# Rotary embedding with the sine ahead of the swap, and fixed PSUM bank pairs for even and odd score tiles and for the row maxima, in the order maximum, scores, scores, maximum

## The chip, the cores and the metric

The program runs on one core of one Trainium2 chip. The metric is the device time of one launch in microseconds (us). TensorE (PE) multiplies and writes to PSUM; VectorE (DVE), ScalarE (ACT) and GpSimd (POOL) do the elementwise work; SyncE (SP) issues the DMAs. Each engine works through its own instructions in order and waits on semaphores that the others count up.

## The reference

A block of two expert layers with attention between them, on x of 8 x 1024 tokens x 256 in float32:

```python
x = x + 0.5 * ffn(layernorm(x))          # 8 experts, top 2, and a shared one
x = x + attention(layernorm(x))
x = x + 0.5 * ffn(layernorm(x))
```

The change touches the attention alone:

```python
c_q, c_kv = h @ w_down_q.T, h @ w_down_kv.T               # 256 -> 128
q, k, v = (c @ w_up.T for each)                            # 16 heads of 64
e, o = xr[..., 0::2], xr[..., 1::2]                        # q and k, all 64 dimensions
rot = stack([e * cos - o * sin, e * sin + o * cos], -1)
attn = softmax(einsum('bhqd,bhkd->bhqk', q, k) / 8)
out = einsum('bhqk,bhkd->bhqd', attn, v) @ w_out.T + residual
```

## The kernel before, in words

Three blocks follow each other: `ffn`, `attention`, `ffn`. In the attention the work goes by pairs of heads, n = 0 to 63 (8 batches x 8 pairs). The rows of a pair's two heads lie on partitions 0 to 63 and 64 to 127, so a product over the 64 dimensions of a head uses half of the array and both heads run beside each other. "Even" and "odd" below are even and odd n.

A pair takes 8 periods, r = 0 to 7. `order` (L701 to L713) writes all steps of all engines in one list, and each engine takes from it those that concern it. Steps that belong to the beginning, the early part, the late part or the end of a period are put there by `at` (L661 to L699). A period holds:

- two score tiles (L894), here s0 and s1, each 128 keys x 512 queries x 2 heads, six row pairs of matmuls in all: the float32 product is made of three products of high and low parts;
- two maxima tiles (L873), here m0 and m1, of the pair that comes next: 128 queries x 512 keys x 2 heads from the high parts alone. DVE takes the row maximum (L1072). The maxima of 512 queries become a row, go to DRAM and back broadcast (`SH`), and are filled into a PSUM bank pair (L1001 on ACT, L1078 on DVE for every fourth tile) ahead of the scores, which add onto them;
- ACT's exponential of each score tile (L1010, `grown`), then two products with V (L905, attends, of the period before), and POOL's sums of exponentials (L1170);
- one or two other steps that share the single bank `OT`: raise (L852, the up projection of q or k, four per pair, in periods 2 to 5, for the pair two ahead or so), value (L864, periods 1 and 6), row (L880, periods 1 and 5), sum (L927, periods 2 and 6), and outward (L945, the output projection). Outward steps stand in odd pairs only: two in period 0, early and late, and one late in periods 3 and 4. Turn and latent (L834, L842) prepare the next batch; the last latent stands late in period 0 of one even pair per batch.

The rotation, one half of q or k at a time: PE raises into `OT`; ACT copies `OT` to `R` (L984); DVE multiplies `OT` by the cosine into `U` (L1049), and waits for ACT's copy first; two DMAs write `R` to `VT` with even and odd rows exchanged; POOL multiplies `VT` by the signed sine (L1149, "sine", end of the next period); DVE adds it to `U` (L1062, "rotate", late in the period after that). When all four are in, ACT makes the high parts `KH` (early in period 0) and `QH` (end of period 0) (L990), POOL the low part of k (L1160), DVE the low part of q, `QL` (L1067, end of period 1).

Score and maxima tiles share three bank pairs `PS0` to `PS2` in turn, in the order in which they stand: `ring = Banks(3, ...)` (L805). Each use takes the pair that the use three before it had, and waits until that one was read: a score tile by its exponential, a maxima tile by its row maximum. PE's wait is in `take`:

```python
before = ring.before[use]
if before:
    pe.wait_ge(*(grown if before[0] == "score" else most_out)(*before[1:]))
```

In the order s0, s1, m0, m1 the use three before m1 is s0 of the same period.

Of the kernel before, what the change touches and what calls it, by code (L numbers as in the profile page):

```python
# [5 lines left out]
class Once:  # L6


    def __init__(self, eng):
        self.eng, self.seen = eng, {}  # L10
# [7 lines left out]
class Signal:  # L18
# [14 lines left out]
    def past(self, *key):  # L33

        return self.sem, self.at.get(key, 0)

# [9 lines left out]
def macaron_kernel(nc, a, out):  # L46
# [557 lines left out]
    def attention(src, dst, held):  # L604
        with ExitStack() as local:
# [3 lines left out]
            def sig(name, by=1):  # L609
                return Signal(ctx.enter_context(nc.semaphore("at" + name)), by)  # L610
# [10 lines left out]
            U = sb("U", [128, 2, S], fp32)  # L621
# [92 lines left out]

            def events(*names):
                return [step[1:] for step in order if step[0] in names]
# [30 lines left out]
            sined, rotated = (sig(x).expect(events("rotate")) for x in ("sined", "rotated"))  # L747
# [47 lines left out]
            def place(use):  # L795
                return room.get(use, OT[:, :])
# [8 lines left out]
            ring = Banks(3, [s for s in order if s[0] in ("score", "most")])  # L805

            def tensor(pe):
# [6 lines left out]
                def take(use):  # L814

                    before = ring.before[use]
                    if before:
                        pe.wait_ge(*(grown if before[0] == "score" else most_out)(*before[1:]))
                    else:
                        for i in (2 * ring.of[use] + 6, 2 * ring.of[use] + 7):  # L820
                            pe.wait_ge(*FREED[first[i][0]](*first[i][1:]))
                    return PS[ring.of[use]]
# [127 lines left out]
            def scalar(act):  # L950
                for step in order:
# [26 lines left out]
                    elif name == "raise":  # L978
                        _, n, i, t = step
                        k, before = swap_of(n, i, t)  # L980
                        act.wait_ge(*raised(n, i, t))
                        if before:
                            act.wait_ge(*swapped[k](*before))
                        act.eng.activation(R[k][:, :], place(step), ACT.Copy).then_inc(raw.sem)  # L984
# [11 lines left out]
                    elif name == "fill" and filler(step[3]) < 2:  # L996
                        _, n, t, j = step
                        before = ring.before[("score", n, t, j)]
                        act.wait_ge(*shift[t](n))
                        act.wait_ge(*(grown if before[0] == "score" else most_out)(*before[1:]))  # L1000
# [23 lines left out]
            def vector(dve):  # L1024
                for step in order:
# [16 lines left out]
                    elif name == "raise":  # L1042
                        _, n, i, t = step
                        sl = slice(t * 512, (t + 1) * 512)
                        dve.wait_ge(*raw(n, i, t))
                        dve.wait_ge(*ups(1))
                        dve.wait_ge(*high.past(n - 1, i))
# [8 lines left out]
                    elif name == "rotate":  # L1056
                        _, n, i, t = step
                        sl = slice(t * 512, (t + 1) * 512)
                        k, before = swap_of(n, i, t)
# [13 lines left out]
                    elif name == "fill" and filler(step[3]) == 2:  # L1073
                        _, n, t, j = step
                        before = ring.before[("score", n, t, j)]
                        dve.wait_ge(*shift[t](n))
                        dve.wait_ge(*(grown if before[0] == "score" else most_out)(*before[1:]))
# [34 lines left out]
            def gpsimd(pool):  # L1112
# [3 lines left out]
                for step in order:  # L1116
# [27 lines left out]
                    elif name == "sine":  # L1144
                        _, n, i, t = step
                        k, before = swap_of(n, i, t)
                        pool.wait_ge(*ups(1))
                        pool.wait_ge(*swapped[k](n, i, t))
                        pool.eng.tensor_tensor(VT[k][:, :], VT[k][:, :], SIN[:, t * 512:(t + 1) * 512], ALU.mult).then_inc(sined.sem)  # L1149
# [160 lines left out]
```

## Time and profile before

| | |
|---|---|
| median of 3 runs | 4203.93 us (4203.29 to 4210.23) |
| profiled execution | 4204.82 us, span 4202.9 us |
| TensorE clock, mean granted | 0.986 |
| busy: PE, DVE, ACT, POOL | 94%, 71%, 66%, 72% of the span |
| attention stage, 1200 to 2200 us | PE 949, DVE 757, ACT 726, POOL 824 us busy |
| DVE row maxima L1072 | x1024, 1220 ns each |
| DVE rotate L1062 | x256, 1385 ns each in the larger group |
| POOL sine L1149 | x254 in the larger group, 1303 ns each |
| ACT copy to R L984 | x252, 597 ns each |

The busy share of PE is modelled at its ends; in the timeline the start of one matmul and the start of the next tell more than the durations. A row of the timeline holds several instructions of one kind when they follow each other.

### The profile page before, as it was taken

The page shows a single profiled execution, that of the slowest core. Times are in us where ns is not written, and L with a number is a line of the kernel's source. Part 1 is how long each engine was busy: PE and PEld are TensorE (multiplying, and loading weights), DVE is VectorE, ACT ScalarE, POOL GpSimd, SP SyncE. Part 2 cuts the span into 40 slices and gives each one's busy share as a digit, 9 for nine tenths or more (in the row PEclk, how much of TensorE's full clock was granted, in tenths as well). Part 3 has the DMA queues.
Part 4 walks back from the last instruction along what each step waited for, and adds up shares of the span by engine and source line. Part 5 has one row for each costly group of instructions (what it writes and reads, how often), then busy time and mean ns, then how long its engine had stood idle before and what let it go on. Part 6 is the DMA issues. An engine that isn't in the chain of part 4 may idle for free. (4 is left out here: it accounts for less than half of the span.)

```text
span 4202.9 us, 66226 instructions
## 1 busy us (share of the span) xinstructions
PE 3943.4 (94%) x24908; PEld 2235.9 (53%) x24908; DVE 2964.9 (71%) x3709; ACT 2769.4 (66%) x3532; POOL 3018.6 (72%) x1634
## 2 busy tenths in 40 slices
PE   7999979999999999999999999999999999989999
PEld 6888834444444444444444444444444444468888
DVE  5656568777777776877777777777777877555563
ACT  4444457777777777777777777777776777744544
POOL 3444458888888887888788788888887888734443
PEclk9999989999999999999999999999999999999999
DMA  3333221112211211121122112111211121133331
GB/s 110 106 121 112 73 91 54 57 54 67 71 52 52 79 54 52 60 78 51 52 65 69 53 56 81 52 51 59 74 55 57 58 72 62 42 110 105 121 111 61
DMA packets 192775, 300.39 MB, mean 71 GB/s; under 512 B 50327, under 2 KB 100936, under 8 KB 191816
## 3 DMA queue, kind: packets, MB, share of 16 engines
q1 hardware_dynamic: 192456, 296.17, 21.9%
q8 instruction: 196, 3.21, 0.3%
q14 instruction: 123, 1.01, 0.1%
HBM read 201.20 MB, written 26.73 MB: 54 GB/s over the span
## 5 line engine op out<-in xcount | busy, mean ns | idle before, releaser
L1072 DVE TENSOR_REDUCE atNM<-atPS 128x2 f32<-128x1024 f32 x1024 | 1208.0, 1220 | 568.5 <-PE atPS L873 563.0
L1170 POOL TENSOR_TENSOR atACC<-atACC,atPT 128x1024 f32<-128x1024 f32 x510 | 1277.2, 2504 | 69.0 <-ACT atPT L1010 15.0
L1010 ACT ACTIVATE atPT<-atPS 128x1024 f32<-128x1024 f32 x1024 | 995.3, 1022 | 197.3 <-PE atPS L894 187.3
L905 PE MATMUL atPO<-atPT,atV 128*64 128x512 f32 x4096 | 972.5, 595 | 0.0
L1001 ACT ACTIVATE atPS<-atSH 128x1024 f32<-128x1024 f32 x768 | 767.5, 1023 | 39.7 <-DMA atSH<-atMD 24.9
L1170 POOL TENSOR_TENSOR atACC<-atPT 128x1024 f32<-128x1024 f32 x255 | 624.7, 2450 | 105.7 <-PE atOT L927 102.8
L873 PE MATMUL atPS<-atKH,atQH 64*128 64x512 f32 x2048 | 456.5, 448 | 124.0 <-ACT atPT L1010 112.3
L1149 POOL TENSOR_TENSOR atVT<-atVT,atSIN 128x512 f32<-128x512 f32 x254 | 331.0, 1303 | 295.9 <-DMA atVT<-atR 295.9
L905 PEld LDWEIGHTS atPO<-atPT,atV 128*64 128x64 f32 x4096 | 281.6, 137 | 472.9 <-issue 466.6
L894 PE MATMUL atPS<-atQH,atKL 64*128 64x512 f32 x2048 | 469.0, 454 | 38.0 <-ACT atPS L1001 35.2
L894 PE MATMUL atPS<-atQH,atKH 64*128 64x512 f32 x2048 | 405.3, 391 | 0.0
L894 PE MATMUL atPS<-atQL,atKH 64*128 64x512 f32 x2048 | 404.7, 391 | 0.0
L894 PEld LDWEIGHTS atPS<-atQH,atKL 64*128 64x128 f32 x2048 | 191.8, 184 | 381.9 <-ACT atPS L1001 174.1
L873 PEld LDWEIGHTS atPS<-atKH,atQH 64*128 64x128 f32 x2048 | 193.7, 185 | 364.9 <-ACT atPT L1010 321.0
L523 POOL TENSOR_TENSOR f2GL<-f2GF,f2GH 128x512 fp32r<-128x512 f32 x144 | 200.6, 1395 | 254.2 <-ACT f2GH L368 254.2
L523 POOL TENSOR_TENSOR f1GL<-f1GF,f1GH 128x512 fp32r<-128x512 f32 x144 | 198.4, 1381 | 251.0 <-ACT f1GH L368 249.4
L1062 DVE TENSOR_TENSOR atU<-atU,atVT 128x512 f32<-128x512 f32 x254 | 351.7, 1385 | 20.6 <-POOL atVT L1149 20.6
L1078 DVE COPY atPS<-atSH 128x1024 f32<-128x1024 f32 x256 | 311.4, 1217 | 11.2 <-ACT atPT L1010 11.2
L984 ACT ACTIVATE atR<-atOT 128x512 f32<-128x512 f32 x252 | 150.5, 597 | 182.5 <-PE atOT L852 182.5
L945 PE MATMUL atOT<-atWO,atAT 128*64 128x256 f32 x1984 | 239.8, 384 | 1.1 <-POOL atAT L1155 1.1
L476 DVE TENSOR_TENSOR f2GF<-f2HB,f2GB 128x512 f32<-128x512 f32 x128 | 101.6, 794 | 182.0 <-ACT f2HB L362 131.7
L1022 ACT ACTIVATE atRSUM<-atOT 128x512 f32<-128x512 f32 x126 | 75.4, 598 | 234.0 <-PE atOT L927 234.0
(280 smaller groups left out, 6835.9 us busy)
## 6 DMA issues: line engine op xcount, KB each, us to landing
atSH<-atMD SPq DMA_DIRECT2D x128, 512.0 KB, 4.5
atVT<-atR SPq DMA_DIRECT2D x508, 128.0 KB, 2.1
f1GB<-f1GD SPq DMA_DIRECT2D x128, 256.0 KB, 7.2
f2GB<-f2GD SPq DMA_DIRECT2D x128, 256.0 KB, 6.9
atRSUM<-atRD SPq DMA_DIRECT2D x126, 256.0 KB, 4.0
X<-x SPq DMA_DIRECT2D x4, 1024.0 KB, 6.0
XS<-x SPq DMA_DIRECT2D x16, 256.0 KB, 3.9
x<-X SPq DMA_DIRECT2D x16, 256.0 KB, 2.7
```

Of the source, the lines that this page charges most:

```text
L523: pool.eng.tensor_tensor(GL[n % NH][:, :], GF32[n % NH][:, :], GH[n % NH][:, :], ALU.subtract).then_inc(low_h.sem)
L873: ins = pe.eng.matmul(bank[:, h, :], QH[n % 2][HI[h], q * 128:(q + 1) * 128], KH[n % 2][HI[h], t * 512:(t + 1) * 512], start=True, stop=True)
L894: ins = pe.eng.matmul(bank[:, h, :], kk[HI[h], keys], q[HI[h], sl], start=False, stop=k == 2, skip_group_check=True)
L905: ins = pe.eng.matmul(PO[HI[h], :], V[n % 2][:, j, HI[h]], PT[k % NPT][:, h, :], start=j == 0, stop=j == T - 1)
L945: ins = pe.eng.matmul(place(step)[HI[c], i * D:(i + 1) * D], AT[:, (n - GP + 1 + q) % NAT, tok:tok + 64], WO[:, (p - GP + 1 + q) * D:(p - ...
L1001: act.eng.activation(PS[ring.of[("score", n, t, j)]][:, :, :], SH[t][:, :, :], ACT.Copy).then_inc(filled[filler(j)].sem)
L1010: act.eng.activation(PT[k % NPT][:, :, :], PS[ring.of[step]][:, :, :], ACT.Exp, scale=SCALE).then_inc(grown.sem)
L1062: dve.eng.tensor_tensor(U[:, i, sl], U[:, i, sl], VT[k][:, :], ALU.add).then_inc(rotated.sem)
L1072: dve.eng.tensor_reduce(NM[:, q // 4, :, q % 4, t], PS[ring.of[step]][:, :, :], AX.X, ALU.max, negate=True).then_inc(most_out.sem)
L1078: dve.eng.tensor_copy(PS[ring.of[("score", n, t, j)]][:, :, :], SH[t][:, :, :]).then_inc(filled[2].sem)
L1149: pool.eng.tensor_tensor(VT[k][:, :], VT[k][:, :], SIN[:, t * 512:(t + 1) * 512], ALU.mult).then_inc(sined.sem)
L1170: pool.eng.tensor_tensor(total[:, :, :], begun[:, :, :], PT[k % NPT][:, :, :], ALU.add).then_inc(gathered.sem)
```

## The change

Two edits, independent of each other.

The rotation: DVE multiplies `OT` by the sine straight into `R` (in ACT's place), then `OT` by the cosine into `U`; the swap follows; POOL subtracts `VT` from `U` ("rotate", at the end of the period after the raise, where "sine" stood). The sign of the table goes with the row it is multiplied in, hence the subtraction. ACT's copy, the step "sine" and DVE's addition are gone.

The banks: even score tiles always use `PS0`, odd ones `PS1`, maxima `PS2`. Each use waits for the last reader of its own pair. The order in a period becomes m0, s0, s1, m1.

```diff
+class Kept:
+    def __init__(self, of):
+        self.of, self.before, last = of, {}, {}
+        for use, bank in of.items():
+            self.before[use] = last.get(bank)
+            last[bank] = use
...
-                    at(end, m, k - 5, ("sine", m, i, t))
-                    at(late, m, k - 4, ("rotate", m, i, t))
+                    at(end, m, k - 5, ("rotate", m, i, t))
...
-                order += begin.get(g, []) + scores + mosts + early.get(g, []) + fills + attends
+                order += begin.get(g, []) + mosts[:1] + scores + mosts[1:] + early.get(g, []) + fills + attends
...
-            ring = Banks(3, [s for s in order if s[0] in ("score", "most")])
+            ring = Kept({s: s[3] % 2 if s[0] == "score" else 2 for s in order if s[0] in ("score", "most")})
+            def cleared(use):
+                before = ring.before[use]
+                if before:
+                    return [(grown if before[0] == "score" else most_out)(*before[1:])]
+                return [FREED[x[0]](*x[1:]) for x in first[6:] if first.index(x) // 2 - 3 == ring.of[use]]
...
-                    elif name == "raise":            # scalar
-                        _, n, i, t = step
-                        k, before = swap_of(n, i, t)
-                        act.wait_ge(*raised(n, i, t))
-                        if before:
-                            act.wait_ge(*swapped[k](*before))
-                        act.eng.activation(R[k][:, :], place(step), ACT.Copy).then_inc(raw.sem)
...
                     elif name == "raise":            # vector
-                        dve.wait_ge(*raw(n, i, t))
+                        k, before = swap_of(n, i, t)
+                        dve.wait_ge(*raised(n, i, t))
                         dve.wait_ge(*ups(1))
+                        if before:
+                            dve.wait_ge(*swapped[k](*before))
+                        dve.eng.tensor_tensor(R[k][:, :], place(step), SIN[:, sl], ALU.mult).then_inc(raw.sem)
                         dve.wait_ge(*high.past(n - 1, i))
                         dve.wait_ge(*(klow if i else qlow).past(n - 1))
                         dve.eng.tensor_tensor(U[:, i, sl], place(step), COS[:, sl], ALU.mult).then_inc(cosine.sem)
...
-                    elif name == "rotate":           # vector
-                        dve.wait_ge(*sined(n, i, t))
-                        dve.wait_ge(*cosine(n, i, t))
-                        dve.eng.tensor_tensor(U[:, i, sl], U[:, i, sl], VT[k][:, :], ALU.add).then_inc(rotated.sem)
...
-                    elif name == "sine":             # gpsimd
-                        pool.wait_ge(*swapped[k](n, i, t))
-                        pool.eng.tensor_tensor(VT[k][:, :], VT[k][:, :], SIN[:, t * 512:(t + 1) * 512], ALU.mult).then_inc(sined.sem)
+                    elif name == "rotate":           # gpsimd
+                        pool.wait_ge(*swapped[k](n, i, t))
+                        pool.wait_ge(*cosine(n, i, t))
+                        pool.eng.tensor_tensor(U[:, i, sl], U[:, i, sl], VT[k][:, :], ALU.subtract).then_inc(rotated.sem)
```

TensorE around the border of periods 0 and 1 of an even pair. `KH0,atQH0` is the pair whose maxima end, `KH1,atQH1` the next one, whose high parts are made in period 0. Before:

```order
L873 MATMUL atPS1<-atKH0,atQH0 128x512 x2
L873 MATMUL atPS2<-atKH0,atQH0 128x512 x2
L905 MATMUL atPO<-atPT4,atV1 64x512 x2
L905 MATMUL atPO<-atPT5,atV1 64x512 x2
L894 MATMUL atPS0<-atQH0,atKL0 128x512 x2
L894 MATMUL atPS0<-atQL0,atKH0 128x512 x2
L894 MATMUL atPS0<-atQH0,atKH0 128x512 x2
L894 MATMUL atPS1<-atQH0,atKL0 128x512 x2
L894 MATMUL atPS1<-atQL0,atKH0 128x512 x2
L894 MATMUL atPS1<-atQH0,atKH0 128x512 x2
L873 MATMUL atPS2<-atKH1,atQH1 128x512 x2
L873 MATMUL atPS0<-atKH1,atQH1 128x512 x2
```

The same place after the change (the maxima are L885 there, the attends L917, the scores L906, the value step L876):

```order
L885 MATMUL atPS2<-atKH0,atQH0 128x512 x2
L917 MATMUL atPO<-atPT0,atV1 64x512 x2
L917 MATMUL atPO<-atPT1,atV1 64x512 x2
L885 MATMUL atPS2<-atKH1,atQH1 128x512 x2
L906 MATMUL atPS0<-atQH0,atKL0 128x512 x2
L906 MATMUL atPS0<-atQL0,atKH0 128x512 x2
L906 MATMUL atPS0<-atQH0,atKH0 128x512 x2
L906 MATMUL atPS1<-atQH0,atKL0 128x512 x2
L906 MATMUL atPS1<-atQL0,atKH0 128x512 x2
L906 MATMUL atPS1<-atQH0,atKH0 128x512 x2
L885 MATMUL atPS2<-atKH1,atQH1 128x512 x2
L876 MATMUL atOT<-atWV,atCKV1 64x128 x8
```

The first maxima tile of the next pair moved from behind the six score products of period 1 to in front of them, and both maxima tiles of a period lie in `PS2`.

VectorE from period 0 to period 2 of an even pair, before (L1078 is a fill, L1083 the step "minus", L1054 the copy of V):

```order
L1078 COPY atPS2<-atSH0 128x1024
L1083 TENSOR_REDUCE atMC<-atNM 128x8
L1072 TENSOR_REDUCE atNM<-atPS0 128x2
L1072 TENSOR_REDUCE atNM<-atPS1 128x2
L1054 COPY atV1<-atOT 128x512
L1067 TENSOR_TENSOR atQL1<-atU,atQH1 128x1024
L1072 TENSOR_REDUCE atNM<-atPS1 128x2
L1072 TENSOR_REDUCE atNM<-atPS2 128x2
L1049 TENSOR_TENSOR atU<-atOT,atCOS 128x512
L1078 COPY atPS1<-atSH0 128x1024
```

And after the change:

```order
L1080 COPY atPS1<-atSH0 128x1024
L1085 TENSOR_REDUCE atMC<-atNM 128x8
L1074 TENSOR_REDUCE atNM<-atPS2 128x2 x2
L1063 COPY atV1<-atOT 128x512
L1069 TENSOR_TENSOR atQL1<-atU,atQH1 128x1024
L1074 TENSOR_REDUCE atNM<-atPS2 128x2 x2
L1055 TENSOR_TENSOR atR0<-atOT,atSIN 128x512
L1058 TENSOR_TENSOR atU<-atOT,atCOS 128x512
L1080 COPY atPS1<-atSH0 128x1024
```

The order is the same but for the sine product in front of the cosine product; `QL` still stands right ahead of period 2's two row maxima.

## Rows read from the trace of the kernel before

**Rows 1.** The page: busy time, share and instructions of each engine.

```profile
PE 3943.4 (94%) x24908; PEld 2235.9 (53%) x24908; DVE 2964.9 (71%) x3709; ACT 2769.4 (66%) x3532; POOL 3018.6 (72%) x1634
```

**Rows 2.** Waits of the whole span: waiter, releaser, us in total, times, longest.

```profile
PEld atPS L873 <- ACT atPT L1010: 321.0, 504, 1.3
```

**Rows 3.** Timeline, period 3 of an odd pair: start, duration, engine, line, idle before.

```profile
2107.05 0.50 PE L894 MATMUL atPS<-atQH,atKL 64*128 64x512 f32 x2
...
2108.54 0.40 PE L873 MATMUL atPS<-atKH,atQH 64*128 64x512 f32 x2
...
2108.98 2.36 DVE L1072 TENSOR_REDUCE atNM<-atPS 128x2 f32<-128x1024 f32 x2 [2.08 <-PE atPS L873]
2109.12 0.51 PE L873 MATMUL atPS<-atKH,atQH 64*128 64x512 f32 x2 [0.19 <-ACT atPT L1010]
2109.56 1.08 PE L852 MATMUL atOT<-atCKV,WK 128*64 128x512 f32 x4
...
2110.47 1.89 PE L905 MATMUL atPO<-atPT,atV 128*64 128x512 f32 x8
...
2111.32 0.69 DVE L1049 TENSOR_TENSOR atU<-atOT,atCOS 128x512 f32<-128x512 f32 x1
2112.19 1.90 PE L945 MATMUL atOT<-atWO,atAT 128*64 128x256 f32 x16
...
2114.01 0.50 PE L894 MATMUL atPS<-atQH,atKL 64*128 64x512 f32 x2
2114.13 0.69 DVE L1110 TENSOR_TENSOR XS<-XS,atOT 128x512 f32<-128x512 f32 x1 [2.12 <-PE atOT L945]
```

**Rows 4.** Timeline, a maxima tile that is first in its run, and its reader.

```profile
2049.99 0.51 PE L873 MATMUL atPS<-atKH,atQH 64*128 64x512 f32 x2
```

```profile
2050.53 2.36 DVE L1072 TENSOR_REDUCE atNM<-atPS 128x2 f32<-128x1024 f32 x2 [5.05 <-PE atPS L873]
```

**Rows 5.** Timeline of DVE, then of PE: periods 4 and 5, even pair.

```profile
2070.70 1.22 DVE L1078 COPY atPS<-atSH 128x1024 f32<-128x1024 f32 x1
...
2073.24 0.18 DVE L1097 TENSOR_REDUCE atRI<-atRQ 128x16 f32<-128x32 f32 x1
...
2073.64 2.35 DVE L1072 TENSOR_REDUCE atNM<-atPS 128x2 f32<-128x1024 f32 x2
```

```profile
2072.77 0.74 PE L873 MATMUL atPS<-atKH,atQH 64*128 64x512 f32 x4
2073.44 1.08 PE L852 MATMUL atOT<-atCQ,WQ 128*64 128x512 f32 x4
...
2076.65 0.27 PE L880 MATMUL atOT<-ident,atMC 128*8 128x128 f32 x1 [0.41 <-DVE atU L1049]
```

**Rows 6.** The line of QL: ns min/median/max, first and last start; then timeline rows.

```profile
L1067 DVE TENSOR_TENSOR atQL<-atU,atQH x64: 1215/2824/3435, 558.7 to 3605.3; 128x1024 fp32r<-128x1024 f32 x64
```

```profile
2146.90 2.96 DVE L1067 TENSOR_TENSOR atQL<-atU,atQH 128x1024 fp32r<-128x1024 f32 x1
```

```profile
2146.40 2.37 POOL L1170 TENSOR_TENSOR atACC<-atPT 128x1024 f32<-128x1024 f32 x1
```

**Rows 7.** The group of QL over the span: count, busy us, mean ns.

```profile
L1067 DVE TENSOR_TENSOR atQL<-atU,atQH 128x1024 fp32r<-128x1024 f32 x64 | 166.5, 2602 | 0.0
```

**Rows 8.** Timeline of ACT, then of PE: periods 7, 0 and 1.

```profile
2135.69 1.98 ACT L1001 ACTIVATE atPS<-atSH 128x1024 f32<-128x1024 f32 x2
2138.04 1.94 ACT L1010 ACTIVATE atPT<-atPS 128x1024 f32<-128x1024 f32 x2 [0.38 <-PE atPS L894]
...
2142.23 1.07 ACT L990 ACTIVATE atQH<-atU 128x1024 fp32r<-128x1024 f32 x1
```

```profile
2132.65 0.50 PE L894 MATMUL atPS<-atQH,atKL 64*128 64x512 f32 x2
...
2144.69 1.09 PE L864 MATMUL atOT<-atWV,atCKV 128*64 128x128 f32 x16
```

**Rows 9.** The page's costliest groups: DVE's addition of the rotation, mean ns.

```profile
L1062 DVE TENSOR_TENSOR atU<-atU,atVT 128x512 f32<-128x512 f32 x254 | 351.7, 1385 | 20.6 <-POOL atVT L1149 20.6
```

More of the change, by code:

```diff
@@ L746, in attention @@
             swapped = [sig(f"swap{k}", 32).expect([s for s in events("raise") if swap_of(*s)[0] == k]) for k in range(4)]
-            sined, rotated = (sig(x).expect(events("rotate")) for x in ("sined", "rotated"))
+            rotated = sig("rotated").expect(events("rotate"))
             high = sig("high").expect(events("high"))
@@ L814, in take @@
                 def take(use):
-                    before = ring.before[use]
-                    if before:
[L818 to L821, printed above, removed]
+                    for event in cleared(use):
+                        pe.wait_ge(*event)
                     return PS[ring.of[use]]
@@ L977, in scalar @@
                         act.eng.activation(C[b % 2][i][:, t * 512:(t + 1) * 512], place(step), ACT.Copy).then_inc(latent_out.sem)
-                    elif name == "raise":
-                        _, n, i, t = step
-                        k, before = swap_of(n, i, t)
-                        act.wait_ge(*raised(n, i, t))
-                        if before:
-                            act.wait_ge(*swapped[k](*before))
-                        act.eng.activation(R[k][:, :], place(step), ACT.Copy).then_inc(raw.sem)
                     elif name == "high":
@@ L997, in scalar @@
                         _, n, t, j = step
-                        before = ring.before[("score", n, t, j)]
                         act.wait_ge(*shift[t](n))
-                        act.wait_ge(*(grown if before[0] == "score" else most_out)(*before[1:]))
+                        for event in cleared(("score", n, t, j)):
+                            act.wait_ge(*event)
                         act.eng.activation(PS[ring.of[("score", n, t, j)]][:, :, :], SH[t][:, :, :], ACT.Copy).then_inc(filled[filler(j)].sem)
@@ L1055, in vector @@
                                             OT[:, :].rearrange("p (i d) -> p i d", d=128)).then_inc(value_out.sem)
-                    elif name == "rotate":
-                        _, n, i, t = step
-                        sl = slice(t * 512, (t + 1) * 512)
-                        k, before = swap_of(n, i, t)
-                        dve.wait_ge(*sined(n, i, t))
-                        dve.wait_ge(*cosine(n, i, t))
-                        dve.eng.tensor_tensor(U[:, i, sl], U[:, i, sl], VT[k][:, :], ALU.add).then_inc(rotated.sem)
                     elif name == "qlow":
@@ L1074, in vector @@
                         _, n, t, j = step
-                        before = ring.before[("score", n, t, j)]
                         dve.wait_ge(*shift[t](n))
-                        dve.wait_ge(*(grown if before[0] == "score" else most_out)(*before[1:]))
+                        for event in cleared(("score", n, t, j)):
+                            dve.wait_ge(*event)
                         dve.eng.tensor_copy(PS[ring.of[("score", n, t, j)]][:, :, :], SH[t][:, :, :]).then_inc(filled[2].sem)
@@ L1143, in gpsimd @@
                             then(10, pool.eng.tensor_tensor(B[:, two], A[:, two], NG[:, :], ALU.mult))
-                    elif name == "sine":
+                    elif name == "rotate":
                         _, n, i, t = step
+                        sl = slice(t * 512, (t + 1) * 512)
                         k, before = swap_of(n, i, t)
-                        pool.wait_ge(*ups(1))
                         pool.wait_ge(*swapped[k](n, i, t))
-                        pool.eng.tensor_tensor(VT[k][:, :], VT[k][:, :], SIN[:, t * 512:(t + 1) * 512], ALU.mult).then_inc(sined.sem)
+                        pool.wait_ge(*cosine(n, i, t))
+                        pool.eng.tensor_tensor(U[:, i, sl], U[:, i, sl], VT[k][:, :], ALU.subtract).then_inc(rotated.sem)
                     elif name == "divide":
```

## The prediction, made before the changed kernel ran

> **What bounds the kernel now.** I read the busy line first: PE is busy for 94% of the span, the other engines for at most 72% [rows 1]. Then the waits, for what PE waits for inside the attention: the line that stands out is the second maxima tile, held by ACT's exponential before 504 of its weight loads [rows 2]. Then the timeline of single periods. There PE is a chain without holes but for this one. Period 3 of an odd pair [rows 3] runs: s0 at 0 (2107.05), m0 at 1.49, m1 at 2.07, raise at 2.51, attends at 3.42, outward at 5.14, the next s0 at 6.96. m0 follows the score product before it at the usual 0.23 (six products and the entry of 0.1 make 1.49), but m1 follows m0 by 0.58. Two dense maxima are 0.23 apart: in period 5 of an even pair m0 and m1 together take 2073.44 - 2072.77 = 0.67 until the raise [rows 5], and the raise comes 0.44 after m1 in either case [rows 3]. So each of the 512 periods can lose 0.35 on the shared bank pair, 180 us in all. DVE, ACT and POOL have slack; what matters is whether each is on time for PE in the new order.
>
> **The wait that goes, and the one that comes.** After the change m1 waits for DVE's row maximum of m0, since both lie in PS2. From m0 = 0: m0 is now first in its run behind another kind of matmul; such a tile reaches DVE 0.54 after its start (2049.99 to 2050.53) [rows 4], against 0.44 when it is not first [rows 3]. A row maximum takes 1.22 (two in 2.36, the second starts after 1.18). A release reaches PE after 0.06. m1 can start at 0.54 + 1.22 + 0.06 = 1.82; its place by the order alone is 0.33 + 6 x 0.23 = 1.71. The step behind it then starts at 2.25 or 2.26, not 2.51. So an undisturbed period gains 0.26, not 0.35. For every 0.1 that DVE comes later than 0.54 to m0, PE loses 0.1; from 0.8 on the period is longer than before. Before, DVE could come late by a whole tile without PE noticing, since both maxima came last and their pairs were wanted again only a period later.
>
> So the question is what DVE does at the start of a period. Its list per raise period is: maximum, maximum (next step 1.17 after the second's start), sine product, cosine product (0.60 each to the next step, as the one with the cosine now, 0.69 in itself), fill (1.13) in every second period. The sine product reads OT in PSUM as the cosine product does, so I price it at the same row. The second maximum starts at 1.82 + 0.54 = 2.36, the sine at 3.53, the cosine at 4.13, OT is free at 4.82, a fill ends DVE's list at 5.86. PE: raise 2.25, attends 3.16 (0.91 on), next s0 or m0 at 4.98 without a late step; with outward, which wants OT, 4.88 by the order and 5.00 by OT (0.18 from the cosine's end, as 2111.32 + 0.69 to 2112.19), so there 0.12 of the gain is gone.
>
> **Period by period** (plus is slower; per pair of heads).
> - Periods 3 and 4 of even pairs and period 6 of all: DVE on time. -0.26 each, 128 periods: -33 us.
> - Period 7, for 39 of 64 pairs (the others below): -10 us.
> - Periods 3 and 4 of odd pairs: period 3 -0.26 + 0.12. In period 4 the addition of the outward step before comes first, 0.12 after the period's border for 0.60 (2114.01 to 2114.13) [rows 3]: maximum at 0.72, m1 at 2.00, +0.18, with the 0.12 of OT that is +0.05. Together -0.09 x 32: -3 us.
> - Period 5, odd: addition until 0.72, then the sums' inverse and "minus", 0.40 from 2073.24 to 2073.64 [rows 5] and some 0.6 where a release is late, say 0.45: maximum at 1.17, m1 at 2.45, next step 2.88 against 2.51: +0.37 x 32 = 12 us.
> - Period 5, even: the fill ends at 5.86, 0.88 into the period, inverse and minus to 1.33, m1 at 2.61, next step 3.04: +0.53. But before, PE already lost 0.4 to 0.5 in many of these, as the row waited for OT (2076.65) [rows 5]; there DVE still had its addition L1062 ahead of the maxima. I put that old loss at 0.35 on the mean of the 32, which leaves +0.18, 6 us.
> - Period 2, all pairs: QL stands ahead of m0's maximum. It starts 1.06 ahead of the border (m1 of period 1 at 1.82, V copied by 4.1, the border at 5.2). It takes 1.2 to 3.4, mean 2.60 [rows 6, 7]. The row of 2146.90 shows why: POOL's sum runs until 2148.77 and QL ends at 2149.86, 1.09 after it [rows 6]; QL does its 1.2 us of work when POOL's instruction is through. At the mean it ends at 1.47, m1 starts at 2.75, the next step at 3.18, against 2.51 and some 0.09 that a late DVE already costs here: +0.58 x 64 = 37 us.
> - Periods 7 to 1 in the 25 even pairs whose period 0 has no late outward or latent. The next pair's QH is ready only at the end of period 0. m0 stood behind 1.49 us of scores, now it stands in front and holds them all. ACT's chain doesn't get shorter: from s0 of period 7 (2132.65) fills are done at 2137.67, QH at 2142.23 + 1.07 = 2143.30 [rows 8]. That is 10.65 after s0; s0 is 0.33 behind m0 now, but ACT waited 0.38 for the next scores; new: QH at 10.67 from m0. m0 at 10.73, value at 12.98, against 2144.69 - 2132.65 = 12.04: +0.94 x 25 = 23 us.
> - The other 39: in period 0 the second fill of ACT makes s1 late by 0.2 and QH makes m0 late by 0.1, -0.26 goes against them; period 1 has the addition, +0.05. Together +2 us.
>
> Sum: -33 - 10 - 3 + 12 + 6 + 37 + 23 + 2 = +34 us.
>
> **The rest of the rotation.** ACT loses 252 copies of 0.6 (the table of the profile), 150 us, which PE doesn't see: in raise periods ACT is ahead. DVE changes one addition (mean 1.39, it too has two SBUF inputs and waits on POOL) [rows 9] for one product of 0.69; busy time falls by some 175 us but the addition stood late in a period, where it delayed a maximum only as in period 5. POOL has the same count and size. The swap starts after DVE's sine, 1.9 after the raise where ACT's copy ended after 1.73: hidden by a period. POOL's rotate no longer has a DVE step behind it, so KH and QH don't come later. DVE now waits for the swap two raises before: long over. The irregular losses of before (waits of DVE on POOL's sine, fills late behind the addition) are 1 to 3 us per batch and may go; per batch the 8 statistics and 8 aggregates on DVE now stand ahead of m0's maximum, up to 1.8 us. I take -4 us for both; bounds -24 and +14. Sum +30 us: 4204.8 + 30 = 4235 for a profiled execution, whose time lies 0.9 above the median: 4234.
>
> A rule of the Trainium skill bears on QL: SBUF — State Buffer, "Who interferes with whom", says that a DVE instruction with two SBUF inputs contends with a GpSimd instruction that reads SBUF, and that the one issued first holds the shared pair while the other fully blocks. By it the new sine product, with one input in PSUM, is safe, and QL, the one large DVE step left with two SBUF inputs, would wait for anything up to a whole POOL sum. The trace agrees: 1.2 us of work and 3.4 at most.
>
> **Bounds.** QL: 1.22 to 3.44 us [rows 6]; at 1.22 period 2 gains 0.26 (-54 us on the sum), at 3.44 it loses 0.84 more (+54 us). The lag of m0: 0.44 instead of 0.54, were the first tile as quick as the others, is -0.1 in every period: -40 us. Sine product: 0.60 by the cosine's row, 1.39 were it as slow as the addition [rows 9]: four per pair, 0.8 each on OT and on the fill, +60 us at most. I take the first since it has the same operands' places.
>
> **Rivals.**
> 1. QL runs through. POOL today stands idle for DMAs and the sums' release and then works through a backlog when QL comes. Without the wait on two later steps it may have caught up by period 1 and be idle there. For it: the shortest QL took 1.2 us, so POOL is sometimes idle there already [rows 6]. Against: the median is 2.8 and POOL's share is 72%. Decides from the point where QL's mean falls under about 1.9. Full price 54 us: 4180. Faster than before.
> 2. The stalls of before go and the losses are a little smaller, so that it comes out even: period 5 at today's 0.5 and the irregular 24 us back: 4234 - 30 = 4204. For it: rotate's waits on POOL really stand in period 5.
> 3. DVE does not catch up. A late m0 maximum delays m1's and everything behind it; if QL stays near its maximum since POOL is denser, period 2 takes 0.84 more: 4234 + 54 = 4288. For it: one late step makes the next late. Against: periods 6 and 7 have room to absorb it.
> 4. m1 still waits as before. Against: no exponential is in its bank pair any more.
>
> **Chances.** Forecast (sum as above) 0.49, rival 1 0.23, rival 2 0.15, rival 3 0.13. A change of 0.2%, 8.4 us, is about what can be told from none: slower 0.62, within it 0.15, faster 0.23. The range reaches from 4172 to 4285.
>
> **What would show it.** In the profile after: PE L885 waits for DVE L1074 instead of ACT, some hundred us in all, longest in period 2 behind QL (L1069); in even pairs PE stands some 1.9 us ahead of the first maxima tile of period 1, released by ACT's QH; an undisturbed period 6 is 0.26 shorter; L1055 takes 0.69. I would be wrong if QL were often under 1.9 us, if m1 followed the scores at 0.23 everywhere, or if the scores of period 1 started without a gap.

## The result, and the profile after

The changed kernel takes 4176.31 us (median of 4 runs, 4174.45 to 4180.44), the kernel before 4206.96 (4203.29 to 4210.23) beside it: a ratio of 0.9929, 95% interval 0.9912 to 0.9946. It is 0.7% faster, where the forecast was 30 us, also 0.7%, slower. The profiled execution took 4176.75 us, span 4174.8, against 4204.82 and 4202.9: its span is 28.1 us shorter.

The page's busy line of the changed kernel, which answers to [rows 1]:

```profile
PE 3931.6 (94%) x24908; PEld 2268.2 (54%) x24908; DVE 2773.6 (66%) x3709; ACT 2611.1 (63%) x3276; POOL 2975.9 (71%) x1634
```

DVE lost 191 us of work (the forecast said some 175), ACT 158 (150), and PE is still the bound. The waits of the changed kernel (waiter, releaser, us in total, times, longest):

```profile
PEld atPS L885 <- DVE atNM L1074: 308.2, 535, 2.8
...
PE atPS L885 <- ACT atQH L995: 84.7, 34, 7.9
PE atPS L885 <- DVE atNM L1074: 69.4, 89, 2.3
```

ACT's exponential no longer holds m1 [rows 2]; DVE's row maximum does, and ACT's `QH` holds the first maxima tile of period 1. Period 3 of an odd pair, PE and then DVE, which answers to [rows 3] (start, duration, line, idle before):

```profile
2099.76 0.50 PE L885 MATMUL atPS<-atKH,atQH 64*128 64x512 f32 x2
...
2101.58 0.50 PE L885 MATMUL atPS<-atKH,atQH 64*128 64x512 f32 x2
2102.01 1.08 PE L864 MATMUL atOT<-atCKV,WK 128*64 128x512 f32 x4
2102.92 1.89 PE L917 MATMUL atPO<-atPT,atV 128*64 128x512 f32 x8
2104.64 1.91 PE L957 MATMUL atOT<-atWO,atAT 128*64 128x256 f32 x16
2106.47 0.50 PE L885 MATMUL atPS<-atKH,atQH 64*128 64x512 f32 x2
```

```profile
2100.30 1.23 DVE L1074 TENSOR_REDUCE atNM<-atPS 128x2 f32<-128x1024 f32 x1 [0.60 <-PE atPS L885]
2102.12 1.23 DVE L1074 TENSOR_REDUCE atNM<-atPS 128x2 f32<-128x1024 f32 x1 [0.59 <-PE atPS L885]
2103.26 0.68 DVE L1055 TENSOR_TENSOR atR<-atOT,atSIN 128x512 f32<-128x512 f32 x1
2103.86 0.68 DVE L1058 TENSOR_TENSOR atU<-atOT,atCOS 128x512 f32<-128x512 f32 x1
```

m0 reaches DVE after 0.54, m1 follows m0 by 1.82, the raise starts at 2.25, as forecast. The cosine product ends at 2104.54 and outward starts at 2104.64, 1.72 behind the attends as before: `OT` is on time. The period, from m0 to the next m0, takes 6.71 instead of 6.96.

To see where the rest went, I cut each profiled execution at the start of s0 in each of the 512 periods, by the timeline of PE. The table has the sums over the 32 even and 32 odd pairs in us, for the kernel before, and what the change added (period r runs from its s0 to the next, so the last period of the last pair is left out; after the change m0 of the next period lies in it):

| period | even, before | even, change | odd, before | odd, change |
|---|---|---|---|---|
| 0 | 181.3 | +56.2 | 264.2 | -18.8 |
| 1 | 186.9 | +2.5 | 173.5 | -1.0 |
| 2 | 202.5 | +4.9 | 202.2 | -5.4 |
| 3 | 171.1 | -8.3 | 223.6 | -12.0 |
| 4 | 171.3 | -8.6 | 219.5 | -1.9 |
| 5 | 185.2 | +1.6 | 177.7 | +6.0 |
| 6 | 200.3 | -8.7 | 204.0 | -12.9 |
| 7 | 168.9 | -10.3 | 159.0 | -20.4 |

These make -37.1. The first s0 came 11.6 later (592.0 instead of 580.4), and the work behind the last s0 took 2.6 less: -28.1 in all.

### The profile page after: what moved, and what is told of

It reads as the page before. It is cut to its first block and busy times, and to the rows that moved or that the text cites. A ratio compares the mean times of both kernels' runs of the same rounds, so it can differ in the third digit from the quotient of the medians.

```text
span 4174.8 us, 65969 instructions
## 1 busy us (share of the span) xinstructions
PE 3931.6 (94%) x24908; PEld 2268.2 (54%) x24908; DVE 2773.6 (66%) x3709; ACT 2611.1 (63%) x3276; POOL 2975.9 (71%) x1634
## 5 line engine op out<-in xcount | busy, mean ns | idle before, releaser
L1074 DVE TENSOR_REDUCE atNM<-atPS 128x2 f32<-128x1024 f32 x1024 | 1254.5, 1225 | 733.8 <-PE atPS L885 731.8
L1173 POOL TENSOR_TENSOR atACC<-atACC,atPT 128x1024 f32<-128x1024 f32 x510 | 1257.2, 2465 | 105.2 <-ACT atPT L1015 52.1
L917 PE MATMUL atPO<-atPT,atV 128*64 128x512 f32 x4096 | 972.6, 595 | 0.0
L885 PE MATMUL atPS<-atKH,atQH 64*128 64x512 f32 x2048 | 519.1, 502 | 161.5 <-ACT atQH L995 84.7
L885 PEld LDWEIGHTS atPS<-atKH,atQH 64*128 64x128 f32 x2048 | 198.2, 188 | 630.2 <-DVE atNM L1074 308.2
L917 PEld LDWEIGHTS atPO<-atPT,atV 128*64 128x64 f32 x4096 | 281.8, 137 | 474.8 <-issue 451.1
L906 PE MATMUL atPS<-atQH,atKL 64*128 64x512 f32 x2048 | 421.6, 403 | 2.2 <-ACT atPS L1006 2.2
L906 PE MATMUL atPS<-atQH,atKH 64*128 64x512 f32 x2048 | 417.8, 399 | 0.0
L906 PE MATMUL atPS<-atQL,atKH 64*128 64x512 f32 x2048 | 416.3, 398 | 0.0
L1152 POOL TENSOR_TENSOR atU<-atU,atVT 128x512 f32<-128x512 f32 x254 | 325.0, 1280 | 115.4 <-DMA atVT<-atR 114.9
L533 POOL TENSOR_TENSOR f2GL<-f2GF,f2GH 128x512 fp32r<-128x512 f32 x144 | 200.3, 1393 | 251.2 <-ACT f2GH L378 251.2
L1158 POOL TENSOR_TENSOR atAT<-atAT,atRSUM 128x512 f32<-128x512 f32 x126 | 160.0, 1291 | 117.8 <-DMA atRSUM<-atRD 114.3
L906 PEld LDWEIGHTS atPS<-atQH,atKL 64*128 64x128 f32 x2048 | 201.1, 189 | 48.2 <-ACT atPS L1006 22.2
L906 PEld LDWEIGHTS atPS<-atQH,atKH 64*128 64x128 f32 x2048 | 202.1, 188 | 40.9
L906 PEld LDWEIGHTS atPS<-atQL,atKH 64*128 64x128 f32 x2048 | 201.1, 188 | 37.3
```

Of the source, the lines that this page charges most:

```text
L533: pool.eng.tensor_tensor(GL[n % NH][:, :], GF32[n % NH][:, :], GH[n % NH][:, :], ALU.subtract).then_inc(low_h.sem)
L885: ins = pe.eng.matmul(bank[:, h, :], QH[n % 2][HI[h], q * 128:(q + 1) * 128], KH[n % 2][HI[h], t * 512:(t + 1) * 512], start=True, stop=True)
L906: ins = pe.eng.matmul(bank[:, h, :], kk[HI[h], keys], q[HI[h], sl], start=False, stop=k == 2, skip_group_check=True)
L917: ins = pe.eng.matmul(PO[HI[h], :], V[n % 2][:, j, HI[h]], PT[k % NPT][:, h, :], start=j == 0, stop=j == T - 1)
L1074: dve.eng.tensor_reduce(NM[:, q // 4, :, q % 4, t], PS[ring.of[step]][:, :, :], AX.X, ALU.max, negate=True).then_inc(most_out.sem)
L1152: pool.eng.tensor_tensor(U[:, i, sl], U[:, i, sl], VT[k][:, :], ALU.subtract).then_inc(rotated.sem)
```

## The experiments

### Each edit alone

Only the rotation: the changed kernel with banks and order as they were.

```diff
-                order += begin.get(g, []) + mosts[:1] + scores + mosts[1:] + early.get(g, []) + fills + attends
+                order += begin.get(g, []) + scores + mosts + early.get(g, []) + fills + attends
...
-            ring = Kept({s: s[3] % 2 if s[0] == "score" else 2 for s in order if s[0] in ("score", "most")})
+            ring = Banks(3, [s for s in order if s[0] in ("score", "most")])
```

> Only the rotation's edit; banks and order as before. Theory (the rotation's edit ends irregular stalls and lets QL come earlier, the order's edit gives 0.26 per undisturbed period and pays in periods 0, 1, 5): m1's wait of 0.58 stays in every period, but the irregular losses before (about 30 us: late fills in periods 7 and 0, the row of period 5 in even pairs) go. 4165 to 4185 us, ratio to before 0.990 to 0.996, mean of QL under 2.2 us, first score at the same time as before (580 us). Rival (all of the gain is the order's): the ratio is 1.000 within 0.002 and QL keeps 2.6 us.

Only the banks and the order: the kernel before, with `Kept`, `cleared` and the new order.

```diff
-                order += begin.get(g, []) + scores + mosts + early.get(g, []) + fills + attends
+                order += begin.get(g, []) + mosts[:1] + scores + mosts[1:] + early.get(g, []) + fills + attends
...
-            ring = Banks(3, [s for s in order if s[0] in ("score", "most")])
+            ring = Kept({s: s[3] % 2 if s[0] == "score" else 2 for s in order if s[0] in ("score", "most")})
```

> Only banks and order; the rotation as before. Theory: DVE still has its addition, which waits on POOL, late in periods 5 to 7 and so ahead of m0's maximum, and QL keeps about 2.6 us, so the loss that was predicted comes true here: 4230 to 4270 us, ratio 1.006 to 1.016. Rival (the order's edit alone brings the gain): 4165 to 4185 us.

The rotation alone is slower: 4253.97 us, ratio 1.0107 (1.0088 to 1.0127). The banks and the order alone are much slower: 4355.94 us, 1.0352 (1.0333 to 1.0372). Both expectations missed: the rotation was to be faster, and the banks and the order were to lose 1.6% at most. As ratios the two multiply to 1.046; together they give 0.993. The edits are independent in the code, but not in time: each takes away what makes the other slow.

What the rotation costs in the old order stands in its waits, first before, then with the rotation alone:

```profile
PEld atOT L927 <- DVE atU L1049: 56.7, 61, 1.7
PEld atOT L880 <- DVE atU L1049: 66.0, 63, 3.3
```

```profile
PEld atOT L939 <- DVE atU L1058: 84.7, 61, 1.7
PEld atOT L892 <- DVE atU L1058: 81.5, 63, 3.3
```

and in the timeline of its period 2, DVE and then PE:

```profile
2125.32 2.34 DVE L1074 TENSOR_REDUCE atNM<-atPS 128x2 f32<-128x1024 f32 x2
2127.59 0.67 DVE L1055 TENSOR_TENSOR atR<-atOT,atSIN 128x512 f32<-128x512 f32 x1
2128.19 0.67 DVE L1058 TENSOR_TENSOR atU<-atOT,atCOS 128x512 f32<-128x512 f32 x1
```

```profile
2128.91 1.07 PE L939 MATMUL atOT<-atACC,atones 128*32 128x512 f32 x8 [0.82 <-DVE atU L1058]
```

The sine product stands between the maxima and the cosine product, and `OT` comes free 0.6 later than it would without it. The next step that wants `OT` then waits: sum in period 2, row in 5, outward in 3 and 4. By the same cut, these four periods cost +79 us; periods 6, 7 and 0 gave back 29. In the new order DVE has read one maxima tile while PE works on the scores, and periods 2 to 4 of the changed kernel show no such loss.

What the new order costs with the old rotation is seen at the boundary of periods 5 and 6 (DVE, then POOL, then PE):

```profile
2103.52 2.55 DVE L1075 TENSOR_TENSOR atU<-atU,atVT 128x512 f32<-128x512 f32 x1
2105.99 1.21 DVE L1085 TENSOR_REDUCE atNM<-atPS 128x2 f32<-128x1024 f32 x1
```

```profile
2103.12 5.17 POOL L1183 TENSOR_TENSOR atACC<-atACC,atPT 128x1024 f32<-128x1024 f32 x2
```

```profile
2104.08 0.50 PE L886 MATMUL atPS<-atKH,atQH 64*128 64x512 f32 x2
...
2107.26 0.50 PE L886 MATMUL atPS<-atKH,atQH 64*128 64x512 f32 x2 [1.30 <-DVE atNM L1085]
```

DVE's addition of the rotation takes 2.55 here, and 0.69 at 2098.43, one period earlier. It starts 0.40 behind the start of a sum of POOL. It ends at 2106.07, 1.99 behind m0; m1 starts 3.18 behind m0 instead of 1.82. Against the kernel before, period 5 alone costs +97 us there and period 6 +37. The new rotation gives this addition to POOL, where no row maximum stands behind it. This is the value of that edit, and no row of the busy shares shows it.

### The order without the fixed pairs, and the fixed pairs without the order

Both edits, but the three pairs in turn as before, in the new order:

```diff
-            ring = Kept({s: s[3] % 2 if s[0] == "score" else 2 for s in order if s[0] in ("score", "most")})
+            ring = Banks(3, [s for s in order if s[0] in ("score", "most")])
```

> Both edits' order and rotation, but the bank pairs still taken in turn (ring of three in the order m0, s0, s1, m1; m1 then again takes the pair of m0, m0 that of a score tile read long ago). Theory: in the steady part nothing differs from the changed kernel, since m1 waits for m0's maximum in both; at the start, where only maxima run, three pairs in turn save the round trips of one pair, some 12 us: 4160 to 4168 us, ratio 0.989 to 0.991. Rival (fixed pairs matter in the steady part): slower than the changed kernel by over 10 us.

The fixed pairs and the rotation in the old order:

```diff
-                order += begin.get(g, []) + mosts[:1] + scores + mosts[1:] + early.get(g, []) + fills + attends
+                order += begin.get(g, []) + scores + mosts + early.get(g, []) + fills + attends
```

> Fixed bank pairs and the new rotation, but the order scores, scores, maximum, maximum as before. Theory: m1 stands right behind m0 and waits for its maximum, 0.44 + 1.22 + 0.06 us after m0 instead of 0.58: +1.15 us in each of 512 periods, less where ACT bounds: 4650 to 4800 us. Rival (PE's wait is hidden by other work): within 2% of the changed kernel.

With the pairs in turn it is 4158.9 us, 0.9878 (0.9861 to 0.9895): 17 us faster than the change and 1 us below what I expected. Fixed pairs in the old order: 4742.1 us, 1.1265 (1.1239 to 1.1291; two runs). There the second maxima tile has nothing between it and the first:

```profile
2101.84 0.39 PE L885 MATMUL atPS<-atKH,atQH 64*128 64x512 f32 x2
2103.55 0.49 PE L885 MATMUL atPS<-atKH,atQH 64*128 64x512 f32 x2 [1.32 <-DVE atNM L1074]
```

It is 1.71 from one to the other (0.44 + 1.22 + 0.05), and no less in any of the 512 periods. So with the new rotation the order carries the gain, and the fixed pair for the maxima brings none: it needs the new order and does no good in it. The new order with the pairs in turn and the old rotation was not run, so how the loss of the banks and the order alone divides between the two is not shown. With the pairs in turn and the new order m1 still takes the pair of m0, the use three before it; only the next m0 takes the pair of s0 instead. By the cut the version in turn is 15.0 us earlier at its first s0 (577.0), and 8.2 faster from there to the last.

### The start: one pair for the maxima

```diff
-            ring = Kept({s: s[3] % 2 if s[0] == "score" else 2 for s in order if s[0] in ("score", "most")})
+            ring = Kept({s: s[3] % 2 if s[0] == "score" else (2 * s[2] + s[3]) % 3 if s[1] == 0 and s[2] < 6 else 2
+                         for s in order if s[0] in ("score", "most")})
```

> The changed kernel, where the maxima that stand ahead of the first scores (the first six query tiles of pair 0) take the three bank pairs in turn; everything later keeps its fixed pair. Theory (one pair makes each of these maxima wait for the maximum before it, which the changed kernel pays once, at the start): the first score comes at 577 to 580 us instead of 592, the rest is as in the changed kernel: 4160 to 4166 us, ratio to before 0.988 to 0.991. So nearly all of what ring_new_order gained over the changed kernel lies at the start. Rival: the gain of ring_new_order was in the steady part: then 4172 to 4180 us here.

It takes 4158.98 us, 0.9876 (0.986 to 0.9893), the same as with the pairs in turn and 1 us below what I expected. The first pair's maxima have no scores among them, and in the changed kernel each waits for the one before:

```profile
554.42 0.79 PE L885 MATMUL atPS<-atKH,atQH 64*128 64x512 f32 x2 [7.90 <-ACT atQH L995]
556.53 0.80 PE L885 MATMUL atPS<-atKH,atQH 64*128 64x512 f32 x2 [1.32 <-DVE atNM L1074]
```

With the three pairs in turn for the first twelve of these tiles the first s0 starts at 579.6 instead of 592.0, which is 12.4 of the 17.1 us by which the two profiled spans differ. The forecast had no term for the start.

### The first maxima tile of period 1

The version with the pairs in turn, and in period 1 of even pairs without a late step in period 0 the old order again, so that `QH` is wanted after the scores. The edit takes in 24 of the 25 pairs; pair 62, the last, keeps its stall (`n % 8 != 6` leaves it out):

```diff
-                order += begin.get(g, []) + mosts[:1] + scores + mosts[1:] + early.get(g, []) + fills + attends
+                swapped_order = n % 2 == 0 and n % 8 != 6 and r == 1 and n >= 0
+                order += begin.get(g, []) + (scores + mosts if swapped_order else mosts[:1] + scores + mosts[1:]) + early.get(g, []) + fills + attends
```

> ring_new_order, and in period 1 of the 25 even pairs without a late outward or latent step in period 0 the order is scores, scores, maximum, maximum again (m1 then takes the pair of s0). Theory (PE stands 1.9 us ahead of the first maximum because QH is late, and holds the scores with it): the stall ahead of the scores goes, m1's wait of 0.58 comes back there, net 1.0 us x 25: 15 to 26 us faster than ring_new_order, 4133 to 4145 us. The wait of PE for ACT's QH falls from 84 us to under 25. Rival (ACT bounds these periods whatever PE does): within 5 us of ring_new_order.

It takes 4131.55 us, 0.9808 (0.9787 to 0.9828): 27 us faster than the pairs in turn alone, and the lowest median of all. PE's wait for `QH` falls from 84.5 us (34 times) to:

```profile
PE atPS L886 <- ACT atQH L996: 24.8, 10, 7.9
```

Period 0 of even pairs falls from +56.7 to +10.6 against before, 46 us or 1.92 for each of the 24. Period 1 of even pairs takes 5 back and period 2 18: there m1 of period 1, V's copy and `QL` come later, and m0's maximum of period 2 waits behind them.

The forecast priced this stall at 0.94 a pair, on the way from the first tile of period 7 to the value step of period 1. Over the 24 pairs from 2 to 62 that way took 12.73 us on the mean before and 13.92 in the changed kernel: +1.19. Part of the surplus is seen in the changed kernel's PE:

```profile
2125.12 0.50 PE L885 MATMUL atPS<-atKH,atQH 64*128 64x512 f32 x2
...
2135.88 0.79 PE L885 MATMUL atPS<-atKH,atQH 64*128 64x512 f32 x2 [2.45 <-ACT atQH L995]
2136.44 0.65 PE L906 MATMUL atPS<-atQH,atKL 64*128 64x512 f32 x2
2136.87 0.65 PE L906 MATMUL atPS<-atQL,atKH 64*128 64x512 f32 x2
...
2139.36 1.09 PE L876 MATMUL atOT<-atWV,atCKV 128*64 128x128 f32 x16
```

m0 starts 10.76 behind m0 of period 7 (forecast 10.73). But the products behind it stand 0.43 apart, not 0.23, and value comes 3.48 behind m0 instead of 2.25. The granted clock, by windows (start:end, length, busy us of PE, PEld, DVE, ACT, POOL with their instructions, then the clock):

```profile
2129.00:2133.00 4.00, 4.00 (x26) 1.83 (x24) 2.63 (x3) 3.69 (x5) 3.71 (x3) 1.00 0.00 0
2133.00:2136.00 3.00, 0.55 (x4) 0.15 (x2) 1.03 (x2) 2.73 (x4) 3.00 (x2) 0.94 0.00 0
2136.00:2139.00 3.00, 3.00 (x14) 2.50 (x16) 1.23 (x1) 1.01 (x1) 2.99 (x2) 0.50 0.00 0
2139.00:2142.00 3.00, 3.00 (x28) 1.36 (x24) 2.53 (x3) 2.77 (x4) 2.73 (x2) 0.99 0.00 0
```

PE stood idle for 2.45 us, and for the next 3 us the clock was at 0.50, the 1.2 GHz level. This does not follow each time: the 24 stalls are all 2.43 to 2.46 us long, but three or more score products stood 0.43 apart behind 13 of them. Those 13 pairs took 14.34 us on the way above, the other 11 took 13.42.

### POOL's low part of k, and the sums' inverse

Two edits on when DVE and POOL do their part, alone and together with the last one. First POOL's low part of k one period later in the changed kernel, which moves POOL's sums against `QL`:

```diff
-                at(end, m, 0, ("high", m, 0), ("klow", m))
+                at(end, m, 0, ("high", m, 0))
+                at(end, m, 1, ("klow", m))
```

> The changed kernel, with POOL's low part of k moved from the end of period 0 to the end of period 1, behind that period's sums. It changes nothing but what POOL is at when DVE's QL comes. Theory (QL takes 1.2 us and the rest of the POOL instruction that is running, and each 0.1 us of it beyond some 1.9 costs period 2 as much on PE): QL's mean moves by up to 0.8 us either way and the time follows it, 64 x the change where it rises, some half of that where it falls; without a change of the mean (within 0.1) the time stays within 6 us of the changed kernel. Rival (QL's length is not what sets period 2): the mean moves by over 0.3 us and the time does not follow.

It takes 4163.93 us, 0.9899 (0.9882 to 0.9915). Period 2 takes 8.0 us less than in the changed kernel, and `QL` takes 1.79 on the mean instead of 1.95. The intervals of this and of the changed kernel overlap, so a gain of 12 us in the whole is likely and not shown.

The inverse of the sums behind period 5's step instead of ahead of m0's maximum, first on the version with the pairs in turn:

```diff
-                at(end, m, 20, ("inverse", m))
+                at(late, m, 21, ("inverse", m))
```

> ring_new_order with the step inverse (two small DVE steps) from the end of period 4 to the late part of period 5, behind the two maxima and the products. Theory (what stands on DVE ahead of m0's maximum is paid by PE one to one): 0.4 us less in period 5 of each pair, up to 25 us: 4135 to 4150 us. Rival (the division on POOL then comes late and outward waits, or inverse was hidden): within 5 us of ring_new_order or slower, with POOL waiting longer for RSUM.

It takes 4178.11 us, 0.9926 (0.9911 to 0.9942): slower by 19, as the rival in the expectation had it. Period 5 did gain 18.9 us as wanted, but period 7 lost 20.5 and period 2 19.7, where `QL` went from 1.80 to 2.08. The inverse goes out to DRAM and back to POOL, which waits for it:

```profile
POOL atAT L1158 <- DMA atRSUM<-atRD: 220.2, 56, 5.9
```

The wait was 123.5 us before this edit. That POOL is behind afterwards, and so late for periods 7 and 2, is my reading and was not traced. Then this edit and the one of period 1 together:

> Both edits on ring_new_order. Theory: they touch different periods and add: 4110 to 4130 us, ratio to before 0.977 to 0.982. Rival: no better than the better of the two.

It takes 4142.26 us, 0.9842 (0.9828 to 0.9857): better than the inverse alone, but 11 worse than period 1's alone; the two do not add as expected. And period 1's with POOL's low part of k later:

> rn_behind with POOL's low part of k moved behind the sums of period 1. Theory: QL's mean falls by 0.1 to 0.2 us and period 2 with it, on top of rn_behind's gain: 4118 to 4130 us, ratio to before 0.977 to 0.981. Rival (in rn_behind POOL meets QL at another phase, and the move changes nothing or harms): ratio above 0.981.

It takes 4137.05 us, 0.9829 (0.9814 to 0.9843), no better than without (0.9787 to 0.9828): these two do not add up either. There period 2 of even pairs takes 228.4 us: in the 24 pairs `QL` starts 1.12 us ahead of s0 of period 2 instead of 1.4 to 1.5, and over all pairs it takes 2.01.

## Why the prediction was wrong

The forecast was +30 us for a profiled execution; it came out at -28, so the direction was wrong. Term by term (us, from the table above; the forecast's terms are rounded and add up to 29):

| term | forecast | measured |
|---|---|---|
| periods 3 and 4, even | -17 | -16.9 |
| period 6, all | -17 | -21.6 |
| periods 7, 0 and 1, all | +15 | +8.2 |
| periods 3 and 4, odd | -3 | -13.9 |
| period 5, odd | +12 | +6.0 |
| period 5, even | +6 | +1.6 |
| period 2, all | +37 | -0.5 |
| rest of the rotation, irregular waits | -4 | in the rows above |
| start | 0 | +11.6 |
| behind the last score | 0 | -2.6 |

**The mechanism was right.** m1 at 1.82, the step behind at 2.25, the gain of 0.26 in an undisturbed period (the median of period 6 is 5.99 against 6.25), `QH` ahead of m0 of period 1: each of these came as forecast.

**The step that failed is period 2.** It said of `QL`: "It takes 1.2 to 3.4, mean 2.60", and "At the mean it ends at 1.47, m1 starts at 2.75, the next step at 3.18". 2.60 is the mean in the kernel before [rows 7]. `QL` after the change, its source line and its group (busy, mean ns):

```profile
L1069 DVE TENSOR_TENSOR atQL<-atU,atQH x64: 1215/1740/3242, 559.9 to 3580.9; 128x1024 fp32r<-128x1024 f32 x64
```

```profile
L1069 DVE TENSOR_TENSOR atQL<-atU,atQH 128x1024 fp32r<-128x1024 f32 x64 | 124.9, 1952 | 0.0
```

With 1.95 the same working has `QL` end at 0.82 (as there, counted to the start of DVE's next step, which the rows show 0.08 ahead of `QL`'s end), m1 at 2.10 and the next step at 2.53. That is -0.07 a pair against before, and -0.01 was measured. So 38 of the 58 us are this one duration.

The other versions with the new order bear it out. Mean of `QL`, and period 2 over all pairs, in us: 1.79 and 396.2 (`klow_later`), 1.80 and 397.0 (`ring_new_order`), 1.95 and 404.2 (the change), 2.00 and 409.5 (`bank_only`), 2.02 and 406.8 (`start_fix`), 2.08 and 416.7 (`rn_inverse`). Each 0.1 of `QL` goes with some 5 to 7 us here, where 0.1 in each of the 64 pairs makes 6.4.

Its length depends on the POOL instruction that is running. Alone it takes 1.22 us; in 62 of the 64 pairs it met a running POOL instruction and ended 1.08 to 1.09 us behind the end of that one. The row of before shows a `QL` that starts 0.50 behind the start of a sum and takes 2.96 [rows 6]. In the changed kernel (DVE, then POOL):

```profile
2141.21 1.38 DVE L1069 TENSOR_TENSOR atQL<-atU,atQH 128x1024 fp32r<-128x1024 f32 x1
...
2186.18 1.87 DVE L1069 TENSOR_TENSOR atQL<-atU,atQH 128x1024 fp32r<-128x1024 f32 x1
```

```profile
2129.45 4.89 POOL L1173 TENSOR_TENSOR atACC<-atACC,atPT 128x1024 f32<-128x1024 f32 x2
...
2139.13 5.71 POOL L1173 TENSOR_TENSOR atACC<-atACC,atPT 128x1024 f32<-128x1024 f32 x2
...
2184.59 5.69 POOL L1173 TENSOR_TENSOR atACC<-atACC,atPT 128x1024 f32<-128x1024 f32 x2
```

`QL` starts 2.08 and 1.59 behind the start of a sum of some 2.4, waits for the little that is left, and slips in between two sums; the two then take 5.7 instead of 4.9. This agrees with the Trainium skill, SBUF — State Buffer, "Who interferes with whom": the instruction issued first holds the port pair that the two engines share, and the other is blocked, whichever engine it is.

I treated this duration as a property of the instruction; it is one of where POOL stands at that moment, and the change moves both. The experiments show which edit did it: `QL` takes 2.46 on the mean with the rotation alone, 2.58 with the rotation and the fixed pairs in the old order, 2.00 with the order and banks alone, 1.80 with the rotation, the order and the pairs in turn. It is the order. `klow_later`, which moves POOL alone, brought 1.79 and the 8 us in period 2. The traces show how the two moved, though not why POOL did. In period 1 of odd pairs `QL` started 4.80 us behind s0 before and 4.00 after, since DVE reads m0 while PE is at the scores; the POOL instruction that it met started 4.01 behind s0 before and 2.43 after. So `QL` came 1.6 into it instead of 0.8. With the rotation alone the two stay at 4.80 and 4.08. Why POOL comes earlier with the order stays open.

In the measured time rival 1 was nearest (4180), and my sign of being wrong came true: 42 of the 64 `QL` took under 1.9, where 12 did before. But the reason of the rival, an idle POOL, is not what happened: POOL was idle at the start of two `QL` of 64, and of three before.

**The terms that were too high by less.** Odd periods 3 and 4: I charged 0.12 a period for `OT`, and there was no such wait. Outward starts 1.72 behind the attends in both kernels, so the 0.18 that I took from [rows 3] as the way from the cosine's end to outward was no wait for `OT`; it is 0.10 in the changed kernel. Without that charge the forecast is -0.26 in period 3 and -0.07 in period 4. Measured were -0.38 and -0.06 on the mean; in period 3 the median fell by 0.26 (6.97 to 6.71), so the surplus of 4 us does not lie in the usual period; it was not traced. Period 5, odd: the forecast had m0's maximum at 1.17. The changed kernel's DVE:

```profile
2113.49 0.69 DVE L1112 TENSOR_TENSOR XS<-XS,atOT 128x512 f32<-128x512 f32 x1 [0.91 <-PE atOT L957]
...
2114.50 1.22 DVE L1074 TENSOR_REDUCE atNM<-atPS 128x2 f32<-128x1024 f32 x1
```

m0 was at 2113.37, so the maximum began at 1.13 and m1 at 2.41. That is 0.04 better than forecast for this pair; over the 32 pairs the period lost 0.19, not 0.37, and the rest of that was not traced.

**The irregular waits of before were undersized.** Periods 7 and 0 of odd pairs got 39 us shorter, where I had 10 for the maxima of all pairs and at most 24 for the rest. The rotation alone takes off 23 us there, the order and banks alone 14. I had put the irregular waits of before at 1 to 3 us a batch, without a row for it. The largest of the kind, POOL's for the swap, fell from 295.9 us in all to 114.9; that it is the cause was not tried by itself. Against it, the stall for `QH` cost 1.19 us a pair instead of 0.94, some 6 us more over 24 pairs. Its row, the 12.04 us of one pair [rows 8], was among the shortest of before (12.03 to 14.89), and the slow clock had no term.

## What to carry to other kernels

The duration of an instruction that shares a port with another engine belongs to the phase between the two engines, not to the instruction: when an edit moves either, take it from its shortest to its longest and not at its mean. Price two edits together when one changes what an engine's queue holds ahead of a step that the other makes urgent: here +1.1% and +3.5% made -0.7%. A second tile that shares a buffer with the first can start only after the reader's latency and the reader's duration (1.71 to 1.82 us behind the first here). That is free only if the producer has as much other work between the two; look for the places, like a start, where it has not.

## What the runs showed of the hardware

- A stall of TensorE can cost more than its length. After 2.45 us of idle time the granted clock was 0.50 for 3 us, and the value step came 1.2 us later than by the order. But equal stalls differ: of 24 that lasted 2.43 to 2.46 us in the changed kernel, 13 were followed by three or more score products 0.43 apart and 9 by none. From m0 to the value step it was 3.45 us in the 13 and 2.41 in the other 11. What decides between them no run here shows. Seven stalls of 1.72 us ahead of the same tile, as the one at 2043.47, left all products at 0.23. In the kernel before, and where the stall is taken away (`rn_behind`), no period after pair 0 has three products at 0.43. The mean granted clock of the span is 0.977 in the changed kernel, 0.982 with the pairs in turn, and 0.986 in `rn_behind` as before.
- The lock between DVE and POOL works both ways: two sums of POOL take 4.89 us alone and 5.7 with a `QL` among them, whose own 1.2 became 1.4 to 1.9. DVE's addition of the rotation, which also reads two operands from SBUF, took 2.55 instead of 0.69 when it started 0.40 behind the start of a sum (`bank_only`).
